# Graph attention in two passes: keys and values from one product of 256 columns, and value sums kept in PSUM by block

## What is computed

```
x_j   = x[src] + edge_attr
q     = x[dst] @ wq.T + bq ;  k = x_j @ wk.T + bk ;  v = x_j @ wv.T + bv      (4 heads of 32)
alpha = sum(q * k, per head) / sqrt(32)
a     = softmax of alpha over the edges with the same dst
out[dst] += a * v
```

## Time and profile before

| | |
|---|---|
| median of 3 runs (lowest, highest) | 12023.37 us (12015.92, 12034.72) |
| the profiled execution's own time | 12019.95 us |
| its span, first to last instruction | 12018.1 us |
| mean granted TensorE clock | 0.734 of 2.4 GHz |
| three score passes | 204 to 1245, 1959 to 2999, 3713 to 4765 us |
| three value passes | 1317 to 1665, 3071 to 3419, 4826 to 5174 us |

### The profile page before, as it was taken

How to read it: one execution, slowest core, us unless ns; L and a number is a source line. 1 busy time by engine, 2 the same in 40 slices (tenths; PEclk the granted TensorE clock), 3 DMA queues, 4 the chain that set the end, 5 groups by cost and what they waited for, 6 DMA issues and landing times. The chain is left out here.

```text
span 12018.1 us, 148393 instructions
## 1 busy us (share of the span) xinstructions
PE 6550.1 (55%) x36272; PEld 5479.0 (46%) x36273; DVE 4612.7 (38%) x10118; ACT 2251.5 (19%) x4313; POOL 6209.6 (52%) x6365
## 2 busy tenths in 40 slices
PE   3666786566786665884335334433533443365555
PEld 3555665555765555853323223233323322244443
DVE  4444754444754444752113112211311221135555
ACT  1222552222542222641000000000000000011111
POOL 2666423666414665504663665466366456625553
PEclk6777898777897777996667666666766666677777
DMA  2444322444313443401111111211111121112221
GB/s 75 128 127 127 103 64 69 128 127 125 106 42 88 129 128 105 125 22 42 46 45 61 46 46 36 68 45 46 60 45 45 34 71 46 46 43 77 78 77 55
DMA packets 698434, 894.29 MB, mean 74 GB/s; under 512 B 148417, under 2 KB 443211, under 8 KB 698130
## 3 DMA queue, kind: packets, MB, share of 16 engines
q0 software_dynamic: 198368, 429.61, 13.6%
q1 hardware_dynamic: 498474, 461.96, 12.4%
q10 hardware_dynamic: 1416, 0.86, 0.0%
HBM read 698.72 MB, written 193.14 MB: 74 GB/s over the span
## 5 line engine op out<-in xcount | busy, mean ns | idle before, releaser
L857 POOL DMA_INDIRECT states<-table_typed,tile_idx x2512 | 2415.9, 962 | 1777.8 <-issue 721.2
L840 POOL DMA_INDIRECT states<-table_x,src_idx x2016 | 1980.1, 982 | 1862.7 <-POOLq L82 742.8
L979 PE MATMUL psum<-states,l_sums_select 128*128 x4480 | 905.5, 336 | 1729.7 <-issue 1696.3
L979 PEld LDWEIGHTS psum<-states,l_sums_select 128*128 128x128 f32 x4480 | 777.0, 244 | 1854.3 <-issue 1853.8
L961 DVE SCALAR_TENSOR_TENSOR l_sums_select<-dst_all,pair_start,iota_row 128x512 f32<-128x512 f32 x560 | 402.1, 749 | 2212.5 <-remote 1401.0
L1091 PE MATMUL psum<-ident,select 128*128 128x128 f32 x2016 | 418.3, 344 | 1199.3 <-DVE states L1059 723.4
L840 POOL DMA_INDIRECT l_pass_ring<-table_kv,src_idx x672 | 655.1, 975 | 658.9 <-DVE score L1312 286.3
L1068 DVE TENSOR_TENSOR states<-w,psum 128x512 f32<-128x512 f32 x504 | 345.2, 685 | 1544.0 <-ACT w L1048 969.0
L857 POOL DMA_INDIRECT states<-table_x,tile_idx x628 | 602.1, 959 | 626.2 <-POOLq L82 337.0
L979 PE MATMUL psum<-states,select 128*128 x2240 | 469.4, 348 | 808.8 <-issue 769.4
L944 ACT COPY t<-psum 128x512 f32<-128x512 f32 x50 | 29.3, 585 | 4534.1 <-PE psum L979 2586.3
(11 more groups left out here) (357 smaller groups left out, 11997.4 us busy)
## 6 DMA issues: line engine op xcount, KB each, us to landing
states<-in_edge_attr_dram SPq DMA_DIRECT2D x2016, 64.0 KB
rows_dram<-l_scores_mixT SPq DMA_DIRECT2D x504, 256.0 KB
l_values_ring<-rows_dram SPq DMA_DIRECT2D x504, 256.0 KB
table_typed<-l_rows_rows SPq DMA_DIRECT2D x40, 1024.0 KB, 4.3
states<-table_typed,tile_idx POOLq DMA_INDIRECT x2512
states<-table_x,src_idx POOLq DMA_INDIRECT x2016
l_pass_ring<-table_kv,src_idx POOLq DMA_INDIRECT x672
table_x<-l_rows_rows SPq DMA_DIRECT2D x40, 256.0 KB, 2.3
```

The lines of the kernel that those rows point to most:

```text
L840: pool.indirect_dma_start(out=ring[:, k % REGIONS, u, :], out_offset=None, in_=table, in_offset=at).then_inc(gathered[k % REGIONS], 16)
L857: pool.indirect_dma_start(out=ring[:, k % TILE_RING, u, :], out_offset=None, in_=table, in_offset=at).then_inc(gathered[k % REGIONS], 16)
L979: ins = pe.matmul(to, picked(k)[:, u, :], rows, start=False, stop=True, skip_group_check=True)
```

## The change

In the score pass, one product of 256 columns for each step gives keys and values; ACT copies the values out after the keys, and SP stores these in place of the turned rows. The product's results take two banks for a region, twice; so the queries have two banks in all, once: their product waits for the scores of the region before (`p_score_kept` j instead of j-1). `mixT` has two places instead of four.

In the value pass nothing is projected. DVE makes the selection matrix in one instruction (`make_select`) and weighs three steps of four; POOL copies the weights and weighs the fourth. PE adds into PSUM by block: three blocks of 132 columns to a bank, 14 banks in all (`VALUE_BANKS`) on eight places; ACT copies each out when it is done, and clears six of them for use again. DVE's additions, the two settings to zero and the last addition are gone; eight banks are cleared by PE at the start. PE loads a table entry for each step (where its block lies) and one for each region (how many banks must be clear).

The tables for that are made in `step_tables`: 37 small instructions on DVE ahead of the edge types and two behind them, a store of 2 x 672 numbers to DRAM, and two loads behind it; SP waits for this store too before it loads the other tables.

```diff
@@ step_tables @@
+                        sp.wait_ge(s_value, 1)
+                        sp.dma_start(value_dram.ap().rearrange("a (c k) -> k a c", k=ROW_K), value_i[:]).then_inc(s_row, 16)
+                        sp.wait_ge(s_row, 64)
+                        sp.dma_start(value_plan[:, :, 0:GROUP], by_region[0:1, :, :]).then_inc(s_in, 16)
+                        sp.dma_start(value_plan[:, :, GROUP:], by_region[1:2, :, GROUP - 1:]).then_inc(s_in, 16)
...
+                    for c in range(VALUE_BANKS):
+                        link(dve.tensor_scalar(bank_f[:, 0, :], block_f[:], float(BANK_VALUES * (c + 1)) if c + 1 < VALUE_BANKS else float(BLOCKS + 1),
+                                               None, ALU.is_lt))
+                        link(dve.tensor_reduce(counts[:, c:c + 1], bank_f[:, 0, :], AX_X, ALU.add))
...
@@ gat_score_pass @@
-                                sp.wait_ge(p_spread, region_of(i, r) + 1)
+                                sp.wait_ge(p_valued, region_of(i, r) + 1)
                                 sp.dma_start(rows_dram[bass.ds(region_of(i, r), 1), :, :].rearrange("a p (u f) -> (a p) u f", f=D),
-                                             mixT[:, r, :, :]).then_inc(p_out[r], 16)
+                                             kept[:, r, :, :]).then_inc(p_out[r], 16)
...
-                                act.wait_ge(p_projected, region_of(i, r) + 1)
+                                act.wait_ge(p_keyed, region_of(i, r) + 1)
                                 at_least(act, p_multiplied, region_of(i, r) - 1)
-                                act.copy(key[:, r % 2, :, :], keys(r)).then_inc(p_evacuated, 1)
+                                act.copy(in_pairs(key[:, r % 2, :, :]), made(r)[:, :, :, 0:D]).then_inc(p_evacuated, 1)
+                                if not (isinstance(i, int) and i == 0):
+                                    act.wait_ge(p_out[r], i * 16)
+                                act.copy(in_pairs(kept[:, r, :, :]), made(r)[:, :, :, D:2 * D]).then_inc(p_valued, 1)
...
                                 pe.wait_ge(p_spread, j + 1)
-                                at_least(pe, p_score_kept, j - 1)
+                                at_least(pe, p_valued, j - 1)
                                 for u in range(GROUP):
-                                    pe.matmul(keys(r)[:, u, :], mixT[:, r, u, :], wt[:, WK, :], start=True, stop=True)
+                                    ins = pe.matmul(made(r)[:, u // pair, u % pair, :], mixT[:, r % 2, u, :], both, start=True, stop=True)
+                                ins.then_inc(p_keyed, 1)
+                                at_least(pe, p_score_kept, j)
...
@@ gat_value_pass @@
+                                pool.tensor_copy(msg[:, r, :, D:W], weights)
+                                pool.wait_ge(p_in[r], (i + 1) * 16)
+                                pool.tensor_tensor(msg[:, r, SHARE:, 0:D].rearrange("p u (h e) -> p u h e", h=GAT_HEADS),
...
+                                at_least(dve, p_summed, j - (REGIONS - 1))
+                                make_select(dve, i, r)
+                                dve.wait_ge(p_in[r], (i + 1) * 16)
+                                dve.tensor_tensor(msg[:, r, 0:SHARE, 0:D].rearrange("p u (h e) -> p u h e", h=GAT_HEADS),
+                                                  ring[:, r, 0:SHARE, :].rearrange("p u (h e) -> p u h e", h=GAT_HEADS),
...
+                            act.copy(acc[:, 0:BLOCKS * ACC_W].rearrange("p (b w) -> p b w", w=ACC_W)[:, c * BANK_VALUES:c * BANK_VALUES + n, 0:W],
+                                     psum[:, c % 8, 0:n * W].rearrange("p (b w) -> p b w", w=W)).then_inc(p_drained, 1)
...
+                                entries = by_step(pe, value_row, j * (GROUP + 1), GROUP + 1, 8 * CHUNK)
+                                pe.wait_ge(p_cleared, entries[GROUP].with_bounds(min_val=1, max_val=VALUE_BANKS))
+                                pe.wait_ge(p_selected, j + 1)
+                                pe.wait_ge(p_weighted, j + 1)
+                                pe.wait_ge(p_weight, j + 1)
                                 for u in range(GROUP):
-                                    ins = pe.matmul(sums(r, u), select[:, r, u, :], msg[:, r, u, :], start=True, stop=True)
+                                    to = banks[:, bass.ds(entries[u].with_bounds(min_val=0, max_val=8 * CHUNK - W), W)]
+                                    ins = pe.matmul(to, select[:, r, u, :], msg[:, r, u, :], start=False, stop=True, skip_group_check=True)
```

More of the change, by code:

```diff
@@ L53 @@
 Q_W = D + 4
+BANK_VALUES = 3
+VALUE_BANKS = -(-BLOCKS // BANK_VALUES)
 CHUNK = 512
@@ L997, in gat_score_pass, with made, in_pairs @@
                 part = sb(f"{name}_part", [P, GROUP, GAT_HEADS], F32, tmp)
+                both = wt[:, WK:WK + 2, :].rearrange("p a b -> p (a b)")
                 pair = GROUP // 2
[L1000 to L1006, removed]
+                def made(r):
+                    return psum[:, 2 + 2 * (r % 2):4 + 2 * (r % 2), :].rearrange("p a (b w) -> p a b w", w=2 * D)
+                def in_pairs(ap):
+                    return ap.rearrange("p (a b) f -> p a b f", b=pair)
+                queries = psum[:, 6:8, 0:pair * Q_W].rearrange("p a (b w) -> p a b w", w=Q_W)
+                with block(name, p_selected, p_mixed, p_turned, p_spread, p_keyed, p_valued, p_projected, p_evacuated, p_multiplied, p_scored,
                            p_score_kept, *p_in, *p_out) as b:
@@ L1120, in gat_value_pass @@
                 msg = sb(f"{name}_msg", [P, REGIONS, GROUP, W], F32, tmp)
-                away = w3[:].rearrange("p (a u) f -> p a u f", a=2)
-                def values(r):
-                    return psum[:, (0, 1, 6, 7)[r], :].rearrange("p (u f) -> p u f", f=D)
-                def sums(r, u):
-                    return psum[:, 2 + 2 * (r % 2) + u // 2, (u % 2) * W:(u % 2 + 1) * W]
-                with block(name, p_cleared, p_mixed, p_spread, p_selected, p_weight, p_weighted, p_summed, p_added, p_projected, *p_in) as b:
+                banks = psum[:].rearrange("p a b -> p (a b)")
+                none = ones[:, 0:1].broadcast_to([P, CHUNK])
+                with block(name, p_cleared, p_drained, p_selected, p_weight, p_weighted, p_summed, *p_in) as b:
                     @b.sync
@@ L1232, in body @@
                                 ins.then_inc(p_summed, 1)
-                        project(0, 0)
-                        project(0, 1)
+                        for bank in range(8):
+                            ins = pe.matmul(psum[:, bank, :], blank[:], ones[0:1, 0:1].broadcast_to([1, CHUNK]), start=True, stop=True)
+                        ins.then_inc(p_cleared, 1)
                         turns(pe, body)
```

148 lines of the change are left out of this document (64 added, 84 removed).

## The result

The changed kernel takes 12078.08 us (median of 5 runs, 12064.08 to 12083.37) against 12023.37 us (the kernel before, now five runs too, 12014.27 to 12034.72): **ratio 1.0044, 95% interval 1.0031 to 1.0056**, slower by 55 us where the prediction had it faster by 58. The profiled execution spans 12077.9 us against 12018.1.

The account below looks back on a forecast made before the run. It took a loop of two regions, just above POOL's floor, to pace the score pass and PE to bound the value pass; -195 + 131 + 6 = -58 us gave 11965 us, range 11700 to 12300.

Parts of the forecast that it names:

- faster by 58: Whole kernel: value passes -195 us, score passes +131, step tables +6, sum -58 us; forecast's chance 0.38.

## What to carry to other kernels

When a change lets an engine address memory by loaded values, count each load on that engine's queue, with the duration of its like in the trace, before anything else; then read them in blocks and start each block at a multiple of four words (five words took 0.58 us instead of 1.23, and twenty 1.36). A releaser named by the profile can be merely the last one seen: where two engines each seem to wait for the other, look at the instructions of the queue itself. Where POOL's gathers run back to back, DVE's instructions with two SBUF operands can be on the path although DVE is half idle (here 21 to 64 us of a score pass of 871 to 913).

## What was not expected of the hardware

- A load of words into PE's registers took 0.33 us for four and 0.59 for five from a multiple of four, 1.23 for five from elsewhere, 1.36 for twenty from a multiple of four. The neighbour-sum passes show it too: ten words 1.08 and 2.40 us in turn, and sixteen on DVE 1.10. An estimate that fits all of these: 0.27 to 0.33 us for each four words in a block that starts at a multiple of four, 0.24 us for each word left over, and 0.24 us for every word where it starts elsewhere. The Trainium skill ("DMA: Bandwidth & Descriptors", section "Latency and other measured facts") has some 600 ns as the floor of such a load (`tensor_load`); four words are below it here.
- A gather that starts beside a DVE instruction with two SBUF operands took up to 1.47 us instead of 0.945, and the stretch alone accounts for the differences between the 36 score passes of the experiments' chips, within 0.6 us of one constant.
- Two DVE instructions of 0.68 us in a row gave a pace of 1.21 us a pair.
- Each 128-column multiplication moved from DVE to POOL made the region 0.07 to 0.08 us longer: DVE's select waits for it.
